# Attention scores on four 64x64 tiles of TensorE, and transpositions of probabilities split by rows

## What is computed

```python
xn = layernorm(x)                                   # x: 8 x 256 x 128
q = rope(heads(xn @ wq.T)); k = rope(heads((xn @ w_kv_down.T) @ w_k_up.T))
scores = q @ k.T / 8 + causal                       # 8 x 16 x 256 x 256
probs = softmax(scores)
s = (probs @ v) @ wo.T                              # v = latent @ w_v_up.T
g = silu(2 * expert(xn, e_star))                    # e_star: the higher of the two best experts
out = x + s * g
```

## Time and profile before

| | us |
|---|---|
| median of 3 runs | 303.01 (302.92 to 303.16) |
| the profiled execution | 303.29 |
| its span, first to last instruction | 301.50 |
| TensorE busy | 289.6 (96%) |
| VectorE, ScalarE, GpSimd busy | 229.7, 239.3, 213.5 |

### The profile page before, as it was taken

One profiled execution on the slowest core, in us unless ns is written; L12 is line 12 of the kernel. 1 busy time (PEld: TensorE's weight loads), 2 busy tenths in 40 slices (PEclk: granted clock), 3 DMA queues, 4 the chain that ended last, 5 costly groups with the idle time before them and its releaser, 6 DMA issues.

```text
span 301.5 us, 8603 instructions
## 1 busy us (share of the span) xinstructions
PE 289.6 (96%) x2362; PEld 235.0 (78%) x2362; DVE 229.7 (76%) x909; ACT 239.3 (79%) x863; POOL 213.5 (71%) x325
## 2 busy tenths in 40 slices
PE   8798999999999999999999989999999999999994
PEld 2576888888888888777776779999977778887663
DVE  4889998987777898988898723444377889898981
ACT  4278789898887889989998676677787898999971
POOL 2478878697778669999999982333226899998730
PEclk9999999999999999999999999999999999999999
DMA  6864685879333233444333382000234243543410
GB/s 192 249 133 115 114 276 148 205 194 300 87 75 68 60 75 83 107 101 102 90 97 90 112 245 55 2 0 2 66 93 108 64 113 99 121 106 109 113 37 17
DMA packets 39596, 33.35 MB, mean 111 GB/s; under 512 B 4801, under 2 KB 36674, under 8 KB 39554
## 3 DMA queue, kind: packets, MB, share of 16 engines
q1 hardware_dynamic: 38098, 30.51, 39.8%
q0 software_dynamic: 1024, 2.10, 2.4%
q10 hardware_dynamic: 432, 0.23, 0.3%
HBM read 11.07 MB, written 4.98 MB: 53 GB/s over the span
## 4 chain that ended last, share of the span: by engine, by line
PE 64%; POOL 14%; DVE 9%; issue 6%; DMA 3%; ACT 1%; POOLq 0%; SPq 0%; DVEq 0%; ACTq 0%
PE bank L1199 9%; PE bank L1187 9%; PE bank L1216 8%; PE bank L1450 7%; PE bank L1438 6%; PE bank L1233 6%; POOL probs L499 5%; POOL staged L488 5%; PE bank L1161 3%; DVE rot_out L617 3%; PE bank L1218 3%; PE bank L1189 3%; POOL xn L515 3%; DMA qk_sb<-staged 3%; DVE masked L633 2%
## 5 line engine op out<-in xcount | busy, mean ns | idle before, releaser
L975 ACT ACTIVATE pexp<-masked,negmax 128x128 f32<-128x128 f32 (+1 forms) x256 | 113.9, 452 | 2.2 <-DVE negmax L633 2.2
L499 POOL TENSOR_SCALAR probs<-pexp,rden 128x128 f32<-128x128 f32 (+1 forms) x195 | 84.3, 447 | 27.0 <-DVE rden L640 25.2
L633 DVE CUSTOM_DVE_ANT_0 masked<-bank,mask 128x128 f32<-128x128 f32 (+1 forms) x256 | 75.9, 352 | 21.4 <-PE bank L1189 20.5
L488 POOL TENSOR_TENSOR staged<-rot_out 128x512 f32<-128x512 f32 x56 | 71.4, 1278 | 16.2 <-DVE rot_out L617 15.6
L617 DVE TENSOR_TENSOR rot_out<-bank,rot 128x1024 f32<-128x1024 f32 x64 | 77.7, 1215 | 4.6 <-PE bank L1163 3.5
L997 ACT COPY probsT<-bank 128x384 f32<-128x384 f32 x126 | 54.0, 480 | 27.3 <-PE bank L1199 26.0
L1199 PE MATMUL bank<-ident,probs 128*128 128x128 f32 x384 | 54.0, 275 | 0.7 <-issue 0.5
L975 ACT ACTIVATION_READ_ACCUMULATOR pexp<-masked,negmax 128x1 f32 x256 | 50.0, 195 | 0.0
L1187 PE MATMUL bank<-qk_sb 64*128 64x256 f32 x256 | 47.0, 428 | 1.7 <-DMA qk_sb<-staged 1.3
L1199 PEld LDWEIGHTS bank<-ident,probs 128*128 128x128 f32 x384 | 43.0, 140 | 3.4 <-issue 1.2
L1233 PE MATMUL bank<-vo_sb,ctxT 128*128 128x128 f32 x256 | 37.8, 278 | 0.7 <-ACT ctxT L1004 0.7
(11 more groups left out here) (117 smaller groups left out, 483.6 us busy)
## 6 DMA issues: line engine op xcount, KB each, us to landing
qk_sb<-staged SPq DMA_DIRECT2D x128, 128.0 KB
w_sb<-in_w SPq DMA_DIRECT2D x2, 1024.0 KB, 5.8
w_sb<-in_w SPq DMA_DIRECT2D x4, 512.0 KB, 5.3
sorted_x<-z SPq DMA_DIRECT2D x1, 1408.0 KB, 8.0
sorted_g<-z SPq DMA_DIRECT2D x1, 1152.0 KB, 5.5
out<-res SPq DMA_DIRECT2D x8, 128.0 KB, 2.3
x_sb<-in_x SPq DMA_DIRECT2D x3, 256.0 KB, 3.8
rot<-in_c_rot SPq DMA_DIRECT2D x1, 512.0 KB, 5.7
```

The lines of the kernel that those rows point to most:

```text
L488: pool.tensor_tensor(staged[:, n % 2, :, m % 2, :], rot_out[:, m % 2, :, 0:S], rot_out[:, m % 2, :, S:2 * S], op=ALU.add).then_inc(staged_ ...
L499: pool.tensor_scalar(probs[:, g % 2, i, c], pexp[:, g % 2, i, c], rden[:, g % 2, i, k:k + 1], 1.0, ALU.mult, ALU.mult).then_inc(probs_read ...
L633: t = dve.tensor_tensor_reduce(masked[:, g % 2, i, c], s_bank[i][:, c], mask[:, c], -1.0, -NEG * 1e8, ALU.add, ALU.min, negmax[:, g % 2, i ...
L975: e = act.activation(pexp[:, g % 2, i, c], masked[:, g % 2, i, c], ACT.Exp, bias=negmax[:, g % 2, i, k:k + 1], scale=-1.0, accum_out=rowsu ...
```

## The change

1. **Scores.** For every step but the first, each head's scores are made of five matmuls with 64 columns of weights each (`SCORE_PARTS`), so that a head's queries use both halves of the columns: 64x64 tiles, four of them. The tokens are taken in four quarters of 64; in the second tile the two quarters change places (`TOKEN_ORDER`), so that the last quarter of the sequence, which needs all 256 keys, shares a column half with the first quarter, which needs 64. Both column halves then have 320 columns of keys for a head, against 384 before.
2. **Token order.** The rotation table and the mask follow the new order, and every sequence is read and written by two DMAs of 64 partitions (`quarter_rows`): 16 DMAs in instead of 5, 16 out instead of 8. Where these are waited for, the counts follow.
3. **Transpositions.** A transposition of 128x128 becomes two of 64 rows each, one in each row half of the array (64x128 tiles), with 64 columns of the identity; rows 0 to 63 go to `t_bank[0]` and rows 64 to 127 to `t_bank[1]`. Each bank now holds halves of both heads, so `turn(g)` waits for both copies of step g-1, and the copies of ACT (in one step of DVE) wait for all twelve transpositions and write 6 runs of 64 columns (`turned_half`).

```diff
+Q = P // 2
+TOKEN_ORDER = (0, 1, 3, 2)
+SCORE_PARTS = ((2, slice(0, S)), (3, slice(0, P)), (1, slice(0, P)), (3, slice(P + Q, S)), (0, slice(0, Q)))
...
+        def quarter_rows(dram, part):
+
+            q = dram.rearrange("b (q p) c -> p b q c", p=Q)
+            return q[:, :, part::3 - 2 * part][:, :, 0:2]
...
+        def turned_half(g, i):
+
+            whole = probsT[:, g % 4].rearrange("p i (k q c) -> p (i k) q c", q=2, c=HD)
+            return whole[:, :, i, :]
...
-                    n = slice(*TURNS[u])
-                    sp.dma_start(x_sb[:, n, :], xv[:, n, :]).then_inc(x_in[u], 16)
+                    for b in range(TURNS[u][0] // 2, TURNS[u][1] // 2):
+                        for part in range(2):
+                            sp.dma_start(x_sb[part * Q:part * Q + Q, 2 * b:2 * b + 2, :],
+                                         quarter_rows(x, part)[:, b]).then_inc(x_in[u], 16)
...
-                sp.dma_start(out[b].rearrange("(n p) c -> p n c", p=P),
-                             res[:, k % 2].rearrange("p (n c) -> p n c", c=C)).then_inc(out_done[k % 2], 16)
+                for part in range(2):
+                    sp.dma_start(quarter_rows(out, part)[:, b],
+                                 res[part * Q:part * Q + Q, k % 2].rearrange("p (n c) -> p n c", c=C)
+                                 ).then_inc(out_done[k % 2], 16)
...
+                act.wait_ge(probsT_done, 2 * g + 2)
                 for i in range(2):
-                    act.wait_ge(probsT_done, 2 * g + i + 1)
-                    act.copy(probsT[:, g % 4, i, :], t_bank[i][:, 0:SW]).then_inc(probsT_ready, 1)
+                    act.copy(turned_half(g, i), t_bank[i][:, 0:SW].rearrange("p (n c) -> p n c", c=HD)).then_inc(probsT_ready, 1)
...
-                for i, r in enumerate(half_rows):
-                    wait(pe, masked_ready, 2 * g - 1 + i if g else 0)
-                    pe.matmul(s_bank[i][:, P:SW], qk_sb[r, 0, p, P:S], qk_sb[r, 1, p, :], start=True, stop=True)
-                for i, r in enumerate(half_rows):
-                    m = pe.matmul(s_bank[i][:, 0:P], qk_sb[r, 0, p, 0:P], qk_sb[r, 1, p, 0:P], start=True, stop=True)
...
+                for k, (q, keys) in enumerate(SCORE_PARTS):
+                    c = half_rows[q % 2]
+                    at = q // 2 * P
+                    for i, r in enumerate(half_rows):
+                        if k == 0:
+                            pe.wait_ge(masked_ready, 2 * g - 1 + i)
+                        m = pe.matmul(s_bank[i][c, at + keys.start:at + keys.stop], qk_sb[r, 0, p, q * Q:q * Q + Q],
+                                      qk_sb[r, 1, p, keys], start=True, stop=True)
                 m.then_inc(scores_done, 1)
 
             def turn(g):
 
+                wait(pe, probsT_ready, 2 * g)
                 for i in range(2):
-                    wait(pe, probsT_ready, 2 * g + i - 1)
                     for k in range(3):
                         if k < 2:
                             pe.wait_ge(probs_ready[i][k], g + 1)
-                        t = pe.transpose(t_bank[i][:, k * P:(k + 1) * P], probs[:, g % 2, i, k * P:(k + 1) * P], ident[:])
+                        for o, r in zip(t_bank, half_rows):
+                            t = pe.transpose(o[:, (3 * i + k) * HD:(3 * i + k + 1) * HD],
+                                             probs[r, g % 2, i, k * P:(k + 1) * P], ident[r, r])
                     t.then_inc(probsT_done, 1)
```

28 lines of the change are left out of this document (18 added, 10 removed).

## The result

The changed kernel takes 306.9 us (305.87 to 309.85, six runs) against 302.97 before: ratio 1.0139, 95% interval 1.0092 to 1.0187. The forecast was 300.6, and its range ended at 305.5. The change makes the kernel slower by 1.4%. Three of all the executions reported here ran over 1.5% above the fastest of their kernel (one of `old_turn_again`, two of `tiles_best_again`); they are in the medians and ranges, but not in the ratios.

A forecast was written before the change was run, and what follows sets the result against it. TensorE (busy 96%) was taken as the bound, with POOL full in the scatter steps. Start +0.7, steps -1.3, -0.3, -0.2, -1.2, -0.5 and end +0.4 gave -2.4: 303.0 to 300.6, own range 299 to 302, wider range 297.5 to 305.5.

The forecast's parts named there:

- TensorE's pieces: Per step on TensorE: scores 0.72 us instead of 0.86, twelve transpositions 0.37 instead of 0.65, each change of tile 0.10.
- Rivals 3, 4 and 5: 3: transpositions load singly, 321.3, chance 0.11; 4: scores' column halves overlap partly, 307, 0.10; 5: they run serially, 331, 0.04.
- the scores' term: Attention steps: scores on four tiles save 0.14 us a step, 19 times in steps 3 to 21.
- the turn's: Steps 3 to 21: split transpositions save 0.28 us, but added tile changes make each turn cost +0.07.
- TensorE full and nobody else: Steps 3 to 21: only TensorE limits, so its savings count in full, -1.3 us.
- Steps 22 to 41: Scatter steps 22 to 37, POOL at 3.44 us against TensorE's 3.465: -0.3; steps 38 to 41: -0.2.
- The gather periods and the last steps: Eight two-step periods, steps 42 to 57, save 0.15 us each, -1.2; steps 58 to 63 save 0.5.
- POOL's need: Gather periods: POOL needs between 6.25 and 6.72 us per two steps, limiting the saving to 0 to 0.28.
- ACT's later copies: After each turn ACT's first copy starts 0.75 us after the turn's start, 0.17 later; costs part of steps 58 to 63.
- Start and end: Split loads delay the start by 0.7 us (0.45 to 1.0); the last result's two DMAs add 0.4.
- The clock: A lower TensorE clock, among unseen things given chance 0.02 together; it had stayed at 1.00 throughout.
- rival 2: No change, 303.0: POOL gives nothing in gather periods, ACT's lateness takes the last steps, start and end cost 1.5; chance 0.14.

The follow-up runs named there:

- old_turn_again: `old_turn` unchanged, run on another chip: 302.45 us, ratio 0.9986.
- tiles_best_again: Repeat, on another chip, of `old_turn` with two gathers moved back two places and second halves of first two loads and last store on ScalarE's queue: 304.97, ratio 1.0080.
- old_turn: The changed kernel with transpositions and their copies as before, keeping four-tile scores and the new token order: 305.23 us, ratio 1.0090.
- again: The changed kernel once more, unaltered, for a second profile: 306.26 us, ratio 1.0133.
- third: The changed kernel once more, unaltered, on another chip: 307.61 us, ratio 1.0135.
- new_turn: The kernel before with only the row-split transpositions and the copies that wait for both halves: 305.62 us, ratio 1.0098.
- new_turn_again: `new_turn` repeated on another chip: 305.93 us, ratio 1.0101.
- after_gather_order: The changed kernel with two gathers moved back by two places: 303.15 us, ratio 1.0036.
- order_only: The kernel before with only the exchanged token order, its two tables and the split loads and stores: 305.18 us, ratio 1.0100.

## Why the prediction was wrong, step by step

**TensorE's pieces: right.** Scores 0.71 (0.72), twelve transpositions 0.37 (0.37), the tile changes as added. Rivals 3, 4 and 5 fall with this. The sequencer rule that the prediction weighed does not bind here: the Trainium skill, TensorE: Matmul & The Clock Gate, section "Step-by-step: what each phase is for", gives about 62 ns per MATMUL where it is not decoded in hardware. Twelve transpositions in 0.37 us are 31 ns each.

**What of it arrives: the scores' term was too large, the turn's too.** Steps 3 to 21 were to gain 19 x 0.14 from the scores and lose 19 x 0.07 to the turn. The scores alone gain 1.15 and 1.23 (both `old_turn`), 0.06 a step, and the turn alone costs 0.46 and 0.75, 0.02 to 0.04 a step. What failed here is "TensorE full and nobody else": it held at TensorE's old pace. In `old_turn_again` TensorE's busy time from 34 to 103 us falls from 68.66 to 67.43, since projections wait for DVE and scores for staged queries:

```profile
34.00:103.00 69.00, 67.43 (x843) 57.21 (x838) 58.55 (x270) 59.97 (x215) 53.64 (x93) 1.00 0.64 162
```

```profile
PEld bank L1172 <- DVE rot_out L628: 1.6, 5, 0.4
PEld bank L1209 <- DMA qk_sb<-staged: 1.0, 2, 0.8
```

In before the first kind of wait is there for 0.9 us, three times, and the second is not.

That the sum of the stretch came out is luck: the two errors nearly cancel. After, `again` and `third` have -1.40, -0.60 and -1.04, where -1.3 was forecast.

**Steps 22 to 41.** Forecast -0.5. `again` and `third` have -0.7 and -0.6, but after +0.17, and `new_turn` +1.42. There the signals of the split turn are late beside scatters as well (7 of 8 recorded in `new_turn`, 9 of 11 in `new_turn_again`). The waits of `new_turn` from 106 to 160 us:

```profile
DVE masked L638 <- PE bank L1195: 6.6, 8, 1.6
ACT probsT L1003 <- PE bank L1206: 6.2, 10, 1.5
```

In before the same two are 5.1 and 4.7 us, the longest 0.9 and 0.8. But `new_turn_again` has 6.5 and 6.5 and loses only 0.16 in this stretch, so these waits do not explain the +1.42. Some 0.75 of the difference is one step, at 157 to 161 us, in which TensorE stands for 0.7 us before the scores without a releaser that the trace shows. The cause is open.

**The gather periods and the last steps: the step that failed.** The prediction put -1.2 in periods 42 to 57 and -0.5 behind them, and its only limits there were POOL's need and ACT's later copies; that the scores' signal could reach DVE late was no term. The part on POOL was right: where signals are on time, two steps of POOL take 6.5 us, as forecast, where the earlier trace rows showed 6.72. POOL of `old_turn_again`, two gathers one period apart:

```profile
236.78 1.31 POOL L526 DMA_INDIRECT xn<-sorted_g,pos  x1 [0.16 <-issue]
...
243.32 1.33 POOL L526 DMA_INDIRECT xn<-sorted_g,pos  x1 [0.16 <-issue]
```

Steps 40 to 58 of `after_gather_order` gain 1.48, against -1.2. But `again` has +0.90 there, `third` +2.73 and after +2.91. Two things that no term held take the gain: signals that come late (some 2.4 us from step 40 to 58, `again` against `after_gather_order`, and 0.8 more to step 63, where -0.5 was forecast) and, in after and `third`, the fourth gather (1.9 us more). Of the 2.4, 0.65 lie in steps 48 to 50, where the two kernels' gather orders differ as well; `old_turn` against `old_turn_again`, one program, gives 2.1 from step 40 to 58 and 1.0 behind. For the last steps the text feared ACT's late copies alone; the two rows of waits of `old_turn` above, with the old turn and its copies, show DVE's wait for the scores grown most, from 0.7 to 4.5 us.

**Start and end: mis-sized.** Forecast +0.7 and +0.4. Start +0.9 to +1.35, and 1.47 in `order_only`; end +0.6 to +0.8. I took the issue of a half load at the 0.44 us of a whole one; it is 0.6 to 0.7, and the second half is what lands last. That accounts for 1.0 of the 1.5 us by which the first statistics are later; the other 0.5 is open. The +2.10 of `after_gather_order` is a further thing: its clock record has 3.4 us at the 1.2 GHz level from 8.1 us on.

**The clock: unseen.** Given a share of 0.02. After and `third` each have +1.5 us in steps 0 to 3, where `again` has 0.10, and that is the first stretch at the 1.2 GHz level; the second, at 286 us, costs after about 0.5 (`again` against after, steps 58 to 63). What TensorE did ahead of the first does not tell why. It had waited for DVE:

```profile
31.86 0.39 PE L1178 MATMUL bank<-xnT_h,wq_h 128*128 128x256 f32 x1 [1.22 <-DVE rot_out L633]
```

but it did so in `again` (1.23 us) and in before (1.07) as well, where the clock stayed.

A mean granted clock under 0.995 stands in 16 of 34 executions of kernels with the split turn, in 11 of 84 of the other changed ones and in 1 of 81 of before. The split turn is thus tied to it by count, and the other changed kernels have it too (`tiles_best_again` in four of ten); why is open.

**Together**, for the profiled execution: start and end 1.9, clock 2.0, late signals 3.2, fourth gather 1.9, the rest -2.5, in all 6.5; the rest is what the forecast had at -3.5. Without late signals and with the other gather order the change comes to 303.15 against 302.82, which is rival 2's outcome, for rival 2's reason in part: start and end cost 1.6 to 2.1, but the gather periods did give their gain, against that rival.
